# Last expert layer: the router's eight weight columns stay in the array while the tokens move, and the gates of four of five chunks come back from memory in rows

## The reference

```python
logits = flat @ router_w.T                      # 1250 x 768 by 768 x 8
probs = softmax(logits); topk_probs, topk_idx = top_k(probs, 2)
importance = probs.sum(axis=0)                  # over all 1250 tokens
running = 1 + 0.1 * (importance - 1) + 0.01
balanced = topk_probs / running[topk_idx]; balanced /= balanced.sum(-1)
h = silu(einsum('th,eih->tei', flat, w1))       # 8 experts of 128 hidden units
outs = einsum('tei,ehi->teh', h, w2)
combined = (outs[top 2] * balanced).sum()       # and the residual is added
```

## Time and profile before

| | |
|---|---|
| median of 3 runs | 2790.53 us (2786.77 to 2791.95) |
| the profiled execution | 2789.39 us, its span 2787.7 us |
| PE busy | 2659.2 us, 95% of the span |
| DVE / ACT / POOL busy | 1509.8 / 762.1 / 343.0 us |
| last layer on PE | from the first transposes at 2526 us to 2783.8 us |
| router on PE | from 2560.55 us |
| gates begin to be turned on PE | 2611.09 us |

### The profile page before, as it was taken

One profiled execution on the slowest core, in us unless ns is written; L12 is line 12 of the kernel. 1 busy time (PEld: TensorE's weight loads), 2 busy tenths in 40 slices (PEclk: granted clock), 3 DMA queues, 4 the chain that ended last, 5 costly groups with the idle time before them and its releaser, 6 DMA issues.

```text
span 2787.7 us, 27687 instructions
## 1 busy us (share of the span) xinstructions
PE 2659.2 (95%) x11062; PEld 1898.1 (68%) x11062; DVE 1509.8 (54%) x2831; ACT 762.1 (27%) x1292; POOL 343.0 (12%) x199
## 2 busy tenths in 40 slices
PE   6999998889999797999999999999989999999999
PEld 4656666556995697877777775555755786557776
DVE  7933222468973997898778998121242562330211
ACT  0023224103861575222122221420001331432000
POOL 0778787000000000000000000000000000000000
PEclk9999999999999898999999999999999999998999
DMA  9222312534001202300111003100351000221011
GB/s 315 47 27 24 47 2 36 155 108 151 2 16 42 56 1 86 117 1 1 68 64 33 23 23 115 43 0 34 75 157 31 35 1 1 66 79 68 23 34 44
DMA packets 131165, 156.75 MB, mean 56 GB/s; under 512 B 95468, under 2 KB 100422, under 8 KB 129254
## 3 DMA queue, kind: packets, MB, share of 16 engines
q1 hardware_dynamic: 60317, 154.51, 17.8%
q0 software_dynamic: 70720, 0.47, 2.6%
HBM read 112.40 MB, written 42.17 MB: 55 GB/s over the span
## 4 chain that ended last, share of the span: by engine, by line
PE 50%; DVE 7%; ACT 2%; DMA 1%; SPq 1%; issue 1%; DVEq 0%; ACTq 0%
PE psum L490 49%; DVE arena L1695 2%; DMA arena<-residual 1%; SPq L1978 1%; DVE arena L1697 0%; DVE arena L1696 0%; DVE arena L1688 0%; ACT arena L1008 0%; ACT arena L1013 0%; DVE arena L1360 0%; DVE arena L1761 0%; PE psum L501 0%; DVE arena L1229 0%; DVE arena L1694 0%; DVE arena L1687 0%
## 5 line engine op out<-in xcount | busy, mean ns | idle before, releaser
L490 PE MATMUL psum<-arena 128*125 128x384 f32 (+15 forms) x9992 | 2529.8, 414 | 65.8 <-issue 17.6
L490 PEld LDWEIGHTS psum<-arena 128*125 128x125 f32 (+6 forms) x9992 | 1774.7, 191 | 796.4 <-issue 176.7
L1949 POOL DMA_INDIRECT count_matrix<-arena x170 | 338.0, 1988 | 146.7 <-DMA count_matrix<-arena 99.2
L1695 DVE RECIPROCAL arena<-arena 128x500 f32<-128x500 f32 x60 | 196.7, 3278 | 2.1
L1442 DVE CUSTOM_DVE_ANT_0 arena<-arena 125x1250 bf16<-125x1250 bf16 (+1 forms) x100 | 139.3, 1458 | 7.1 <-ACT arena L1041 6.6
L1529 DVE TENSOR_TENSOR arena<-arena 125x1250 f32<-125x1250 f32 x80 | 116.4, 1454 | 23.3 <-ACT arena L988 20.4
L1962 POOL MEMSET arena<- 125x60 f32 x1 | 0.2, 208 | 987.9 <-PE psum L490 987.9
L985 ACT ACTIVATE arena<-arena 125x1250 f32<-125x1250 f32 x80 | 107.0, 1337 | 53.4 <-PE psum L490 53.3
L895 ACT ACTIVATE arena<-psum 128x500 f32<-128x500 f32 (+1 forms) x90 | 39.6, 534 | 299.6 <-PE psum L501 299.4
L1532 DVE SCALAR_TENSOR_TENSOR arena<-arena 125x1250 f32<-125x1250 f32 x80 | 116.9, 1461 | 2.8
L988 ACT ACTIVATE arena<-arena 125x1250 f32<-125x1250 f32 x80 | 105.9, 1323 | 13.5 <-DVE arena L1529 13.5
(11 more groups left out here) (190 smaller groups left out, 1487.9 us busy)
## 6 DMA issues: line engine op xcount, KB each, us to landing
arena<-in_ffn_w SPq DMA_DIRECT2D x3, 4608.0 KB, 14.6
count_matrix<-arena SPq DMA_DIRECT2D x2, 6250.0 KB, 28.8
arena<-in_gat_w SPq DMA_DIRECT2D x5, 2304.0 KB, 9.7
arena<-count_matrix SPq DMA_DIRECT2D x20, 546.9 KB
residual<-arena SPq DMA_DIRECT2D x30, 336.0 KB
arena<-residual SPq DMA_DIRECT2D x30, 336.0 KB
arena<-residual SPq DMA_DIRECT2D x10, 672.0 KB
residual<-arena SPq DMA_DIRECT2D x10, 672.0 KB
```

The costliest lines, as they stand in the source:

```text
L490: return pe.matmul(o, lhsT, rhs, start=start, stop=stop, skip_group_check=share)
L1695: now(dve.reciprocal(t_, t_))
L1949: pool.indirect_dma_start(counts[k], bass.IndirectOffsetOnAxis(ap=IDX_I[0:T, c:c + 1].bitcast(U32), axis=0), COUNT[0:T, c:c + 1], None, co ...
```

## The change

Three things. **The router's product** is turned round: RWT (128 x 8) is the stationary operand and 500, 500 and 250 tokens of XT move, 18 matmuls into three banks with the 8 experts on partitions. DVE copies the three banks to LGT in SBUF, and after half of `up1(1)` PE turns LGT with 10 transposes to the form that DVE needs. **The gates of chunks 1 to 4**: one transpose of all of GG (125 x 80 to 80 x 125), a DVE copy to SBUF, one DMA to a scratch tensor in memory, and four DMAs that read 8000 bytes each (2 tiles x 8 experts x 125 tokens) into every one of the 128 partitions. DVE multiplies the hidden units of these chunks by those buffers. Only chunk 0 still has `gb`. **The waits**: DVE waits for a chunk's gate rows ahead of its multiplication, and `g2` of chunks 1 to 4 waits for a count of finished multiplications in place of a drained bank.

```diff
-    V.append(("router",))
+    V.extend(("router", c) for c in range(3))
+    V.append(("router_turned",))
     A.extend(("g1", 1, i) for i in range(4))
@@ PE
             pe.wait_ge(grw_loaded, 16)
-            b = fill("V", ("router",))
+            for c, (n0, n) in enumerate(CH):
+                b = fill("V", ("router", c))
+                for k in range(KD):
+                    last = mm(b[0:E1, 0:n], RWT[:, k, :], XT[:, k, n0:n0 + n], k == 0, k == KD - 1)
+                last.then_inc(v_filled, 1)
+            up1(1, range(2))
+            pe.wait_ge(v_drained, V_AT[("router", 2)] + 1)
+            b = fill("V", ("router_turned",))
             for t in range(NT):
-                for k in range(KD):
-                    last = mm(b[0:T, t * E1:(t + 1) * E1], XT[:, k, t * T:(t + 1) * T], RWT[:, k, :], k == 0, k == KD - 1)
+                last = pe.transpose(b[0:T, t * E1:(t + 1) * E1], LGT[0:E1, t * T:(t + 1) * T], IDENT[0:E1, 0:E1])
             last.then_inc(v_filled, 1)
-            up1(1)
+            up1(1, range(2, 4))
...
-                if c < 5:
+                if c == 0:
                     pe.wait_ge(gates_made, 1)
+                    b = fill("V", ("gates_turned",))
+                    pe.transpose(b[0:NT * E1, 0:T], GG[0:T].rearrange("p a b -> p (a b)"),
+                                 IDENT[0:T, 0:T]).then_inc(v_filled, 1)
                     for i in range(4):
-                        b = fill("V", ("gb", c, i))
+                        b = fill("V", ("gb", 0, i))
...
                 if c > 0:
-                    pe.wait_ge(v_drained, V_AT[("gb", c - 1, 3)] + 1)
+                    if c == 1:
+                        pe.wait_ge(v_drained, V_AT[("gb", 0, 3)] + 1)
+                    else:
+                        pe.wait_ge(ga_made, c - 1)
@@ DVE
+            for c, (n0, n) in enumerate(CH):
+                dve.wait_ge(v_filled, V_AT[("router", c)] + 1)
+                dve.tensor_copy(LGT[0:E1, n0:n0 + n], bank(("router", c))[0:E1, 0:n]).then_inc(v_drained, 1)
...
+                if c == 0:
+                    dve.wait_ge(v_filled, V_AT[("gates_turned",)] + 1)
+                    b = bank(("gates_turned",))
+                    dve.tensor_copy(GATE_ROWS[0:NT * E1], b[0:NT * E1, 0:T]).then_inc(v_drained, 1)
+                    dve.wait_ge(v_drained, count[0])
+                    dve.engine_nop().then_inc(gate_rows_made, 1)
...
+                elif c < 5:
+                    dve.wait_ge(gate_rows_loaded[c - 1], 16)
                     for i in range(4):
                         dve.wait_ge(a_drained, A_AT[("g1", c, i)] + 1)
...
+                        last = dve.tensor_tensor(o, o, GATE_B[c - 1][:, :, 2 * i:2 * i + 2, :].rearrange("p t e q -> p e t q"),
+                                                 ALU.mult)
+                        if i < 3:
+                            step(last)
+                    last.then_inc(ga_made, 1)
@@ SP
+            def gate_rows(t):
+                if t == 1:
+                    sp.wait_ge(gate_rows_made, 1)
+                    load(gates_dram, GATE_ROWS[0:NT * E1], gate_rows_saved)
+                    sp.wait_ge(gate_rows_saved, 16)
+                    for c in range(1, 5):
+                        rows = gates_dram[2 * c * E1:2 * (c + 1) * E1, :].rearrange("a b -> (a b)").rearrange(
+                            "(o n) -> o n", o=1)
+                        load(GATE_B[c - 1].rearrange("p a b c -> p (a b c)"), rows.to_broadcast([128, 2 * E1 * T]),
+                             gate_rows_loaded[c - 1])
+
+            residual(3, res[X3], SLOT_2, out, gate_rows)
```

More of the change, by code:

```diff
@@ L192, in plan @@
             A.extend(("g1", c, i) for i in range(4))
-        if c < 5:
-            V.extend(("gb", c, i) for i in range(4))
+        if c == 0:
+            V.append(("gates_turned",))
+            V.extend(("gb", 0, i) for i in range(4))
         if c > 0:
@@ L209, in gps_kernel @@
     neg_dram = nc.dram_tensor("neg_saved", [T, NT * N], BF16).ap()
+    gates_dram = nc.dram_tensor("gate_rows", [NT * E1, T], F32).ap()
     res = [nc.dram_tensor(f"residual{i}", [N, D], F32).ap() for i in range(5)]
@@ L414, in gps_kernel @@
         assert G_AT + 7480 <= K_AT
+        LGT = mem(B_AT, N)
+        GATE_ROWS = mem(B_AT + N, T)
+        GATE_B = [mem(at, 2, E1, T) for at in (B_AT + 1400, B_AT + 3400, B_AT + 5400, C_AT)]
         v_filled, a_filled = sem("v_filled"), sem("a_filled")
@@ L460, in gps_kernel @@
         gw1_loaded, gw2_loaded, grw_loaded = sem("gw1_loaded"), sem("gw2_loaded"), sem("grouter_loaded")
+        gate_rows_made, gate_rows_saved = sem("gate_rows_made"), sem("gate_rows_saved")
+        gate_rows_loaded = [sem(f"gate_rows_loaded{i}") for i in range(4)]
+        logits_turned = sem("logits_copied")
         rl_made, re_made, rp_made, gates_made, ga_made = (sem("router_centred"), sem("router_exp"), sem("router_probs"),
@@ L816, in _, with up1 @@
             gat1(3)
-            def up1(c):
+            def up1(c, parts=range(4)):
                 pe.wait_ge(gw1_loaded, 16)
-                for i in range(4):
+                for i in parts:
                     b = fill("A", ("g1", c, i))
@@ L857, in _ @@
                                 last = pe.transpose(b[:, j * 250 + tt * T:j * 250 + (tt + 1) * T],
-                                                    GG[0:T, 2 * c + tt, e:e + 1].to_broadcast([T, 128]), IDENT[0:T, 0:T])
+                                                    GG[0:T, tt, e:e + 1].to_broadcast([T, 128]), IDENT[0:T, 0:T])
                         last.then_inc(v_filled, 1)
                 if c > 0:
-                    pe.wait_ge(v_drained, V_AT[("gb", c - 1, 3)] + 1)
+                    if c == 1:
+                        pe.wait_ge(v_drained, V_AT[("gb", 0, 3)] + 1)
+                    else:
+                        pe.wait_ge(ga_made, c - 1)
                     pe.wait_ge(gw2_loaded, 16)
@@ L1851, in _ @@
             gat1(3)
-            dve.wait_ge(v_filled, V_AT[("router",)] + 1)
-            b = bank(("router",))
+            for c, (n0, n) in enumerate(CH):
+                dve.wait_ge(v_filled, V_AT[("router", c)] + 1)
+                dve.tensor_copy(LGT[0:E1, n0:n0 + n], bank(("router", c))[0:E1, 0:n]).then_inc(v_drained, 1)
+            dve.wait_ge(v_filled, V_AT[("router_turned",)] + 1)
+            b = bank(("router_turned",))
             v = b[0:T, 0:NT * E1].rearrange("p (a b) -> p a b", a=NT)
@@ L1888, in _ @@
             for c in range(6):
-                if c < 5:
+                if c == 0:
+                    dve.wait_ge(v_filled, V_AT[("gates_turned",)] + 1)
[3 more added lines that the diff above has]
+                    dve.engine_nop().then_inc(gate_rows_made, 1)
+                    for i in range(4):
+                        dve.wait_ge(a_drained, A_AT[("g1", 0, i)] + 1)
+                        dve.wait_ge(v_filled, V_AT[("gb", 0, i)] + 1)
+                        b = bank(("gb", 0, i))
+                        o = GA[0][:, 2 * i:2 * i + 2, :]
+                        dve.tensor_tensor(o, o, b[:, 0:500].rearrange("p (a b) -> p a b", a=2), ALU.mult).then_inc(v_drained, 1)
+                elif c < 5:
+                    dve.wait_ge(gate_rows_loaded[c - 1], 16)
                     for i in range(4):
                         dve.wait_ge(a_drained, A_AT[("g1", c, i)] + 1)
[L1892 to L1895, removed]
+                        o = GA[c % 2][:, 2 * i:2 * i + 2, :].rearrange("p e (t q) -> p e t q", t=2)
+                        last = dve.tensor_tensor(o, o, GATE_B[c - 1][:, :, 2 * i:2 * i + 2, :].rearrange("p t e q -> p e t q"),
[3 more added lines that the diff above has]
+                    last.then_inc(ga_made, 1)
                 if c > 0:
@@ L2179, in _ @@
                 sp.wait_ge(y_stored[i], 64)
-            residual(3, res[X3], SLOT_2, out)
+            def gate_rows(t):
[9 more added lines that the diff above has]
+            residual(3, res[X3], SLOT_2, out, gate_rows)
 def _inputs(inputs):
```

## The result

| | before | after |
|---|---|---|
| median of 5 runs | 2790.53 us | 2773.35 us |
| ratio, 95% interval | | 0.994 (0.9925 to 0.9955) |
| profiled execution; its span | 2789.39; 2787.7 us | 2768.79; 2767.1 us |
| PE instructions | 11062 | 10925 |
| router's start to end of the last residual sum | 223.8 us | 207.6 us |

The account below looks back on a forecast made before the run. PE, busy 2659.2 us or 95% of the span, was taken as the bound. Terms of -12.9, -0.2 and -5.1 sum to -18.2 us, from median 2790.53 to 2772.3; own range 2769 to 2775, 8 in 10 for 2767 to 2780.

Parts of the forecast that it names:

- Router and clock behind it: Router's start to DVE's first step on imp: 49.01 us becomes 36.1 with the clock kept up, -12.9 us.
- Turning the logits: Ten added PE transposes in the middle of up1(1): cost taken as 1.07 us, bounds 0 and 2.2.
- The first gates: Gates' first transpose to chunk 0's products: about 3.4 us instead of 3.63, -0.2 us, bounds -0.4 and +0.5.
- the first rival: The clock falls in the gates stretch, costing up to 3.9 us in all: 2776.2 us; chance 20%.
- the new wait for DVE's multiplication: Ahead of chunk 0's first products, PE waits about 1.4 us for DVE, replacing 1.7 us of transposes.
- The later gates: Chunks 1 to 4: three times 1.71 us of transposes leave PE with no new wait, -5.1 us.
- The sum: Whole kernel: -12.9 - 0.2 - 5.1 = -18.2 us, tail unchanged, giving 2772.3 us against the median.
- the main case: Whole kernel: the forecast of 2772.3 us, with no fall of the clock at the gates; chance 65%.
- Eight stationary columns: Rival at the new router: they leave most of the array unused, clock stays low, 25.2 us there, 2787.1 total; chance 10%.
- The rows came back: Rival at chunks 1 to 4: gate rows land late and PE waits 75 us in all, 2848 us; chance 3%.

Follow-up runs that it names:

- e3: The kernel before with its 60 router matmuls unchanged but strewn among the first two banks of up1(1): 2778.95 us, ratio 0.9961.
- e2: The kernel before with only the change's gates part, the router as before: 2783.81 us, ratio 0.9978.
- e5: Changed kernel, each chunk's gate rows read four or eight times, one after another: 206.4 us from router's start to last sum with four, 2843.9 us whole time with eight.

## Why the prediction was right

**Router and clock behind it: forecast -12.9, measured -12.2** (49.01 to 36.82). The last of the three banks reached DVE 12.8 us after the start (12.59). Turning the logits took 1.38 us (11.50 from DVE's last copy to its next step, less two banks of 5.06), within the bounds of 0 and 2.2 but above the 1.07 taken. The rest, from there to `imp`, was 12.52 against 12.32. No wait of ACT or DVE reached PE. That the clock is what was slow, e3 shows directly; the prediction had it from the rows alone. The forecast's own range, 2769 to 2775, also counts in the clock's phase. No run shows that it moves this term: in all three profiles with the slow router (before, its repeat, e2) the clock was low for 27.31 us and the stretch took the same 48.92 us. At the gates it did move the time, by 1.1 or 3.3 us.

**The first gates: forecast -0.2, measured +0.8** in the profiled execution (4.46 us to the first product, where the chain had 3.63; +1.0 if one counts to the product's own start, 2614.55, in before). Without a fall it is 3.32 us (e2 and e5), as worked out; the 0.1 us taken in it for DVE's signal had no row, and DVE was idle for 0.21 us there in both. This is the term that was off, and by the first rival: the clock fell. I gave it 2 in 10, on the ground that the same wait before had done no harm; it came in all four profiles of the changed kernel, though in neither of e5's. Its price was put at up to 3.9 us and was 1.1 or 3.3. The reason named for it was only in part right: the new wait for DVE's multiplication stands behind the transposes, and the clock was down before that wait, and in three of the four before the transposes. The argument "it did no harm in the one profile" was too weak: the fall comes in one kernel and not in another with the same wait, and its length varies between executions (3.41 and 10.24 us at 0.50 in the changed kernel).

**The later gates: forecast -5.1, measured -4.9** (from the first product in the chain to the last sum's start 164.2 us, where it was 169.1; -5.0 with 2614.55 as the start). e2 alone had -5.1 (223.8 to 218.7).

**The sum:** -18.2 against -16.2 in the profiled pair, -14.1 in the executions with the longer fall, -17.4 in e5 with four reads, which had none. The ratio's interval is -20.9 to -12.6 us, and the median lay 1.05 us above the forecast. That the main case's number came out so closely is in part luck. The clock did fall, which that case excluded, and by the stretches the gain was 14.1 us in three of four profiles; the medians differ by 17.2, with single executions of the changed kernel from 2768.79 to 2777.33 us. The mechanism and the terms of the router and of the later gates are shown; the last 3 us of the number are not.

**The rivals that did not come.** Eight stationary columns did not lower the clock (1.00, 5.03 us for six matmuls of 500 columns, 2561.45 to 2566.48 by DVE's copies, the same as with 128 columns). The rows came back in 9 us. Gaps between matmuls were not what lowered the clock at the router: before, there was none (22.00 of 22.00 us busy) with the clock at 0.50, and e3 brought it to 1.00 with the same matmuls. At the gates the clock stood at 1.00 over 17 transposes (e2, e5) and over 32, and in five of six falls it was down before the first of them. Whether the 8-column matmuls of `imp` or the idle 1.6 us behind them weigh more, these runs cannot say.

## What to carry to other kernels

Read the granted clock beside PE's busy share: here a stretch of matmuls with 8 moving columns was 100% busy (22.00 of 22.00 us) at 0.50 of the clock, and spreading it among matmuls of 250 columns won as much as turning the product round, and 0.9 us more. Around the ten matmuls of `imp` and PE's 1.6 us wait behind them the clock fell in all four profiles of the changed kernel and in neither of e5's two, with the same work there, so "it did no harm before" is weak ground, and several profiles are needed before calling a fall absent. Compare stretches behind the change, not whole times, when the two differ by less than the scatter ahead of them.

## What was not expected of the hardware

Reads of the same 8000 bytes into 128 partitions, four issued together, ran at 400 to 464 GB/s (2601 to 2609 us of the changed kernel) and each landed within 10.8 us of its issue; read one after the other, each took 4.65 us on average. The clock stayed at 0.50 with PE and its weight loads busy all the time (22.00 of 22.00 us), and at one place of one program it fell for different lengths, 3.41 and 10.24 us (1.1 and 3.3 us lost).
